# The last layer of a four-layer image network turned round: transposes behind the product, 8x8 patches as partitions, border columns moved by DMA and added by VectorE

## What is computed

```python
# layer 3, x: B x 48 x 256 x 256, _gn: group norm (scale and shift folded into w_in here)
y = einsum('oc,bchw->bohw', w_in, _gn(x))                 # 48 -> 288 channels
yp = y cut into 8 x 8 patches                             # 32 x 32 patches an image
yp = irfft2(rfft2(yp) * fft_mask)                         # per channel, within a patch
y  = depthwise 3 x 3 convolution of the image put together again, zero border
x1, x2 = split(y, 2, axis=1)                              # 144 + 144 channels
out = x + einsum('oc,bchw->bohw', w_out, gelu(x1) * x2)   # 144 -> 48 channels
```

## Time and profile before

| | us |
|---|---|
| median of 3 runs | 12443.44 |
| lowest, highest | 12438.75, 12449.53 |
| span of the profiled execution (no other time is given of it) | 12461.3 |
| of it TensorE busy | 12084.7 (97%) |
| of it VectorE, ScalarE, GpSimd busy | 7757.3, 5633.1, 4999.7 |

### The profile page before, as it was taken

One profiled execution on the slowest core, in us unless ns is written; L12 is line 12 of the kernel. 1 busy time (PEld: TensorE's weight loads), 2 busy tenths in 40 slices (PEclk: granted clock), 3 DMA queues, 4 the chain that ended last, 5 costly groups with the idle time before them and its releaser, 6 DMA issues. The chain is left out here.

```text
span 12461.3 us, 389987 instructions
## 1 busy us (share of the span) xinstructions
PE 12084.7 (97%) x160850; PEld 8648.5 (69%) x160850; DVE 7757.3 (62%) x17493; ACT 5633.1 (45%) x11858; POOL 4999.7 (40%) x4364
## 2 busy tenths in 40 slices
PE   8999999899989999899999999999998999999999
PEld 7877444499977777555555555555557888888887
DVE  0000455444435545788888888888887777777777
ACT  0000111243433333455555555555556777777776
POOL 0000222212420055566666666666663444444444
PEclk9999999999999999999999999999999999999999
DMA  4333465695984587766666666666662222222222
GB/s 142 132 132 132 127 159 154 147 179 89 166 164 146 147 230 199 93 88 87 88 89 88 88 88 88 88 88 87 89 87 67 57 57 57 57 54 56 55 55 52
DMA packets 2289545, 1323.30 MB, mean 106 GB/s; under 512 B 1876085, under 2 KB 2199164, under 8 KB 2202256
## 3 DMA queue, kind: packets, MB, share of 16 engines
q1 hardware_dynamic: 2013196, 1200.80, 49.5%
q10 hardware_dynamic: 275072, 105.14, 3.7%
HBM read 648.82 MB, written 450.45 MB: 88 GB/s over the span
## 5 line engine op out<-in xcount | busy, mean ns | idle before, releaser
L1803 PE MATMUL l_m<-l_wa,l_pix 128*128 128x288 f32 x8192 | 2211.4, 413 | 2.7 <-DVE l_wb L1985 2.7
L1803 PEld LDWEIGHTS l_m<-l_wa,l_pix 128*128 128x128 f32 x8192 | 1475.5, 190 | 688.8 <-issue 361.9
L1659 POOL TENSOR_TENSOR l_qkv<-l_qkv,l_copies 128x576 f32<-128x576 f32 x1024 | 1437.1, 1403 | 631.3 <-DVE l_qkv L1996 621.5
L1649 POOL TENSOR_TENSOR l_pix<-l_raw 128x516 f32<-128x516 f32 x1024 | 1217.1, 1189 | 1042.6 <-DVE l_t L2033 1017.1
L1484 PE MATMUL l1h_ps<-l1h_ring,l1h_w 96*96 96x256 f32 x6120 | 1328.8, 379 | 62.7 <-ACT l1h_ring L1426 60.2
L1484 PEld LDWEIGHTS l1h_ps<-l1h_ring,l1h_w 96*96 96x96 f32 x6120 | 999.8, 163 | 391.5 <-issue 60.4
L2318 PEld LDWEIGHTS l_e<-k_ident,l_turn 128*112 128x112 f32 x9900 | 1069.1, 133 | 173.0 <-issue 110.6
L2318 PE MATMUL l_e<-k_ident,l_turn 128*112 128x128 f32 x9900 | 1158.2, 275 | 11.4 <-ACT l_turn L2403 3.0
L2403 ACT ACTIVATE l_spread<-l_e 112x512 f32<-112x512 f32 (+1 forms) x1584 | 871.7, 569 | 521.4 <-PE l_e L2318 509.5
L1517 DVE SCALAR_TENSOR_TENSOR l1h_ring<-l1h_ps,l1h_bias,l1h_columns 96x256 f32<-96x256 f32 x1020 | 670.4, 657 | 678.4 <-PE l1h_ps L1484 672.7
L517 PE MATMUL l0a_rows<-l0a_x 128*49 128x245 f32 x8144 | 1043.0, 371 | 0.0
(11 more groups left out here) (269 smaller groups left out, 22947.3 us busy)
## 6 DMA issues: line engine op xcount, KB each, us to landing
l0a_x<-x_px_dram SPq DMA_DIRECT2D x128, 1176.0 KB, 5.1
l0b_x<-x_in_dram SPq DMA_DIRECT2D x128, 493.8 KB
l_raw<-l_raw SPq DMA_DIRECT2D x128, 483.6 KB, 7.3
l_raw<-x_dram SPq DMA_DIRECT2D x1270, 48.0 KB, 3.7
l_x<-x3p_dram SPq DMA_DIRECT2D x132, 384.0 KB
l_out<-x_dram SPq DMA_DIRECT2D x528, 96.0 KB, 2.4
out_dram<-l_out SPq DMA_DIRECT2D x132, 384.0 KB, 4.5
x_dram<-l0b_out ACTq DMA_DIRECT2D x256, 193.5 KB, 3.1
```

Source lines behind the costliest of these rows:

```text
L1649: nc.gpsimd.tensor_tensor(pix[:, n % 2, i, half * HALF:(half + 1) * HALF].rearrange("p (r w) -> p r w", w=PW), in0, in1, op).then_inc(pix_ ...
L1659: nc.gpsimd.tensor_tensor(q, q, copies[:, g % 2, 1:2, :].broadcast_to([128, 2, OUTC]), ALU.add)\
L1803: last = nc.tensor.matmul(bank[i][:, 0:OUTC], pix[:, k, i, first:first + 128], wa[:, b, i, :], start=True, stop=(i in (1, 2)))
```

## The change

The product is left as it is, but what follows it is turned round: patches stay partitions through the rim sums, gelu and the product of the halves, and the transposes come last.

- `turn` is now two buffers of 128 partitions (two parts of the channels x 64 patches) by 10 x 10 positions by 2 halves by 24 channels, and positions run along the free axis.
- The border columns lie in neighbouring partitions now. `move_edges` has SP copy them by DMA: for each of the four groups of 32 partitions and each of two sides one transfer from `turn` to `edge`, shifted by one partition, so 31 partitions of 480 values (1920 bytes) each; 8 transfers a third, 24 a band. `add_edges`, on DVE, adds both sides in one instruction.
- GpSimd only adds and saves the border rows, 128 x 768 each; the four short adds a third are gone.
- gelu and the product are two pieces a third (128 x 768) instead of four of 112 x 512. The product goes to `gate`, from which 16 transposes a third (not 50) are made, behind it; ACT alone copies them (`read_rows`, 4 of 128 x 512 a third, in place of the 13).
- `project` is one step a band, of 6 x 4 x 2 = 48 products of 24 rows by 512 columns, not two steps of 12 with 48 rows.
- The constants come without the old permutation of channels.

Cut to its core:

```diff
+            def move_edges(n, j):
+                u = n * 3 + j
+                sp.wait_ge(a_out, conv_at(n, j, COMP))
+                sp.wait_ge(b_out, conv_at(n, j, COMP))
+                if u >= 2:
+                    sp.wait_ge(edged, u - 1)
+                for first in range(0, 128, TX):
+                    here, there = slice(first, first + TX - 1), slice(first + 1, first + TX)
+                    for side, column, dst, src in ((0, 9, there, here), (1, 0, here, there)):
+                        sp.dma_start(edge[dst, u % 2, side, :],
+                                     turn[src, u % 2, column].rearrange("p y g i -> p (y g i)")).then_inc(edge_in[u % 2], 16)
...
             def slab(q, ty, n, first, last):       # SP
                 if not last:
                     load_x(...)
+                move_edges(n, 0)
+                move_edges(n, 1)
                 if not first:
-                    store(n)
+                    store(n - 1)
+                move_edges(n, 2)
                 load_residual(q, ty, n, first)
...
             def slab(q, ty, n, first, last):       # TensorE
                     convolve(n, j)
-                    if j < 2 and not first:
-                        project(n, j)
-                    if j == 2 and not last:
-                        channels(nq, n + 1, False)
-                    transpose(n, j, first)
+                    if j == 0 and not first:
+                        transpose(n - 1, 2, False)
+                    if j == 1:
+                        if not first:
+                            project(n - 1, False)
+                        transpose(n, 0, False)
+                if not last:
+                    channels(..., n + 1, False)
+                transpose(n, 1, last)
...
+            def add_edges(n, j):                    # VectorE
+                u = n * 3 + j
+                tile = turn[:, u % 2].rearrange("p x y g i -> p x (y g i)")
+                dve.wait_ge(a_out, conv_at(n, j, COMP))
+                dve.wait_ge(b_out, conv_at(n, j, COMP))
+                dve.wait_ge(edge_in[u % 2], 128 * (u // 2) + 128)
+                nc.vector.tensor_tensor(tile[:, 1:9:7], tile[:, 1:9:7], edge[:, u % 2], ALU.add).then_inc(edged, 1)
...
             def slab(q, ty, n, first, last):        # VectorE
+                for g in range(COMP):
+                    read_turn(dve, nc.vector.tensor_copy, 1, n, 0, g, b_done, b_out)
+                    if g in (1, 3) and not first:
+                        gated(u - 1, g // 2)
+                for g in range(COMP):
+                    read_turn(dve, nc.vector.tensor_copy, 1, n, 1, g, b_done, b_out)
+                    if g == 1:
+                        add_edges(n, 0)
+                for h in range(2):
+                    gated(u, h)
+                add_edges(n, 1)
+                if not first:
+                    for m in range(4):
+                        residual(n - 1, m)
+                for g in range(COMP):
+                    read_turn(dve, nc.vector.tensor_copy, 1, n, 2, g, b_done, b_out)
+                ...
+                    for g in range(YR):
+                        read_y(dve, nc.vector.tensor_copy, 1, n + 1, g, False, b_done, a_done, b_out)
+                        if g == 5:
+                            add_edges(n, 2)
+                        if g in (4, 7):
+                            gated(u + 1, g // 7)
...
         def _(pool):
-            def join(pairs):
-                s = spread[:, pairs]
-                nc.gpsimd.tensor_tensor(s[:, :, 8, :, 0:TX - 1], s[:, :, 8, :, 0:TX - 1], s[:, :, 0, :, 1:TX], ALU.add)
-                nc.gpsimd.tensor_tensor(s[:, :, 1, :, 1:TX], s[:, :, 1, :, 1:TX], s[:, :, 9, :, 0:TX - 1], ALU.add)
+                    pool.wait_ge(edged, u + 1)
```

More of the change, by code:

```diff
@@ L2116, in stage_l3 @@
     AB = YR + 3 * COMP
[L2117 to L2125, removed]
+    EDGE = 10 * C
+    LANE = 32
+    GROUPS = PX // 4
     with nc.cleanup_on_exit(), ExitStack() as ctx:
@@ new lines, in project @@
+            def project(n, ended):
+                pe.wait_ge(t_out, n * 12 + 12)
+                bank_pair_read(conv_at(n, 2, 5) if ended else conv_at(n + 1, 1, 2))
+                for k in range(6):
+                    j, r = k // 2, k % 2
+                    for m in range(4):
+                        lanes = slice(m * LANE, m * LANE + CH)
+                        for side in range(2):
+                            last = nc.tensor.matmul(e[m][side * HI:side * HI + C, :], wout[lanes, j, r, :],
+                                                    rows[lanes, j, side * 8:(side + 1) * 8, r, :], start=(k == 0), stop=(k == 5),
@@ L2394, in turned_before @@
-        def turned_before(eng, n, j, first):
-            if not (first and j == 0):
-                for k in range(2):
-                    eng.wait_ge(e_done[k], (n * 3 + j) * E[k])
+                    if j == 0 and not first:
[5 more added lines that the diff above has]
+                if not last:
+                    channels(1 if q == 0 and ty == BANDS - 1 else q, n + 1, False)
@@ new lines, in slab, with read_y @@
+                transpose(n, 1, last)
+            slabs(slab)
+            transpose(N - 1, 2, True)
+            project(N - 1, True)
+        def read_y(eng, copy, s, n, g, first, done, other, ready):
+            if g == 0 and not first:
+                eng.wait_ge(other, n * AB)
+            eng.wait_ge(done, n * AB + (g + 1))
+            bank = slots[MIX_SLOTS[g % 4]][s]
+            m0 = s * TX + STARTS[g]
+            copy(y[:, :, m0:m0 + SIZES[g]], bank[:, 0:SIZES[g] * C3].rearrange("p (t c) -> p c t", c=C3)).then_inc(ready, 1)
@@ L2439, in _ @@
+                if last:
+                    for h in range(2):
+                        gelu(u + 1, h)
+                else:
+                    for g in range(YR):
+                        read_y(act, copy, 0, n + 1, g, False, a_done, b_done, a_out)
+                        if g in (3, 6):
+                            gelu(u + 1, g // 6)
+                read_rows(n, 1)
             slabs(slab)
-            for piece in range(4):
-                gelu(2 * BANDS - 1, 2, piece)
+            for h in range(2):
+                gelu(N * 3 - 1, h)
@@ L2476, in residual @@
[L2476 to L2482 removed]
+            dve.wait_ge(blank, 1)
+            dve.sem_inc(blank, 1)
+            for g in range(YR):
+                read_y(dve, nc.vector.tensor_copy, 1, 0, g, True, b_done, a_done, b_out)
```

407 lines of the change are left out of this document (171 added, 236 removed).

## The result

The changed kernel takes 15,973.0 us (median of 4 runs, 15,959.1 to 15,978.0), the kernel before, run beside it, 12,446.5 (12,438.8 to 12,452.1): a ratio of 1.283, 95% interval 1.281 to 1.285. The forecast was 15,930. The profiled execution spans 15,976.0 us.

A forecast was written before the change was run, and what follows sets the result against it. Three serial waits for single-engine edge transfers bound a band: 3 x 23.2 + 23.6 + 5 (clock) = 98.2 us against 45.3; +52.9 over 66 bands adds 3490, giving 15,930 us, range 14,800 to 17,600.

The forecast's parts named there:

- One engine for 31 partitions: Edge transfers: equal shares of partitions put all eight of a set through one DMA engine, 21.1 us a set.
- L: Time from a third's last copy to its landed edges, three times a band: 23.2 us each (20.0 to 33.6).
- Rival 1: Edge pieces spread over all DMA engines, issues bound a set: L 4.6 to 6.7 us, 12,130 us, faster; chance 0.09.
- Rival 2: Each edge transfer has one engine, but a set's eight have different ones: 49.8 us a band, 12,740 us; chance 0.06.
- The piece's time: Edge transfers: one engine takes 85 ns for each 1920-byte piece, with 72 and 127 as ends.
- rival 3: The single engine copies edge pieces at 127 ns: some 17,600 to 18,200 us; chance 0.08.
- Three waits, none beside another: DVE's in-order queue keeps a band's three edge waits from overlapping, so a band lasts at least three times L plus the rest.
- Between the waits: Band work outside the three edge waits: 23.6 us at full clock plus 5 for the clock, 28.6 in all.
- The clock behind the second wait: TensorE's products after edges 1 start at half speed following the pause, adding 2.5 us a band.
- The last part: Edges 2 landed to third 0's last copy in the next band: 5.7 + 6.4 us, plus 1.7 for the clock.
- What the engines alone would allow: Last layer, if only busy times counted: a band falls from 45.3 to about 32 to 37 us.
- The sign for the DMA engines: Last layer's profile: mean share of the DMA engines stays low, near 7% for the edges plus 11 for the rest.

The follow-up runs named there:

- e1: Changed kernel with 30 partitions per edge transfer instead of 31, the last pair of patches of each group left out: 13,245.6 us, ratio 1.064 to the kernel before.
- e2: Changed kernel with each 31-partition edge transfer split into two, of 16 and 15, so sixteen a set: 14,291.4 us, ratio 1.147 to the kernel before.
- e3: Changed kernel with edge transfers of 112 and 15 partitions per side, a mask in VectorE's sums removing cross-strip pairs: 12,612.2 us, ratio 1.013 to the kernel before.
- e5: Changed kernel, same 31-partition transfers, but the wait and the edge sum moved from VectorE's queue to GpSimd's: 14,432.1 us, ratio 1.160 to the kernel before.
- e9: Changed kernel plus 165 and 130 unused identity transposes on TensorE in the waits for edges 0 and 1: 15,945.7 us, ratio 1.280 to the kernel before.
- e4: Changed kernel without the edge transfers and VectorE's wait for them, the sum adding zeros: 12,254.6 us, ratio 0.984 to the kernel before.
- e10: e4 also without the loads of x behind the first band, all bands reading the first band's x: 12,088.3 us, ratio 0.970 to the kernel before.
- e7: e3 with the edge sums placed later in VectorE's queue, behind other copies and the residual: 12,289.1 us, ratio 0.987 to the kernel before.
- e6: Changed kernel with GpSimd adding the edges and ten transfers a set, of 64 and 15 partitions: 12,599.5 us, ratio 1.012 to the kernel before.

## Why the prediction was right

**One engine for 31 partitions: right.** It was read off a share of 45.0% for loads of 49 partitions. After the change the share is 6.6% and the pieces go one at a time. e1 (30 partitions), e2 (16 and 15) and e3 (112 and 15) each cut L, from 22.5 us to 8.7, 13.9 and 5.7 on the mean, with the same or nearly the same bytes. The rule quoted from the Trainium skill ("DMA: Bandwidth & Descriptors", section "Why a DMA increments its semaphore by 16 and not by 1") agrees with all four in how many engines share a transfer; which engines they are, no run shows. Rival 1 (spread, 12,130) and rival 2 (different engines for the eight, 12,740) are refuted by the 1.04 above.

**The piece's time: 79 ns, taken as 85.** It lies near the row of one engine's share that I chose; rival 3's 127 ns, from rows of 16 engines at once, did not come. The first two waits are 1.4 us shorter for it, and the third is 24.0, since the loads of the residual (L2216) are issued while its set is under way: in the set above the step from one piece of the edges to the next is 99 ns from the first of the residual's pieces on, where it was 83 until then. I had said that none of SP's other transfers was in front of a set, which holds; that one could lie beside it I had not counted. The three waits are 2.2 us a band shorter than forecast.

**Three waits, none beside another: right, for the reason given.** TensorE has 64 long waits of each of the three kinds in 64 bands. e5 shows that the order on VectorE makes them add up: off its queue, the same transfers cost 23 us a band less.

**Between the waits: 2.7 us a band too low.** 31.3 us on the mean (4.2 + 10.7 + 16.3) against 28.6, and 32.6 in the band above. That the sum, 98.2, came within 0.5 us of the mean band is luck in part: this error and that of the three waits are of one size and cancel.
- The residual was mis-sized: 4.04 us for four sums, taken as 4 x 0.69 = 2.8 from a line of before. It did not lengthen its part, because TensorE starts after two of the four: the chain has two sums, 2.07 us from 12069.26, and then TensorE at 12071.37. The two that were left out of the path take off more (1.4 us at the forecast's price) than the longer ones put on (0.7 for two).
- The clock behind the second wait was sized right: from 12071.37 to the last copy it is 6.8 us, less 0.7 for that copy 6.1, for which 3.55 + 2.5 were taken. That this adds up is luck in part, since the low clock and the residual's last two sums lie beside each other: the sums end at 12073.30 and TensorE's second group starts at 12073.35, so at full clock the first group would have gained nothing, as e9 shows. Three windows of the changed kernel show 15 us without a product, then the two levels, 0.50 (1.2 GHz) and 1.00:

```profile
12056.00:12071.00 15.00, 0.00 (x0) 0.00 (x0) 2.82 (x3) 0.24 (x1) 1.58 (x1) 0.55 0.05 19
12071.00:12073.00 2.00, 1.63 (x40) 1.63 (x40) 2.00 (x3) 0.00 (x0) 1.07 (x2) 0.50 0.03 8
12075.00:12078.00 3.00, 3.00 (x141) 3.00 (x136) 2.53 (x4) 2.51 (x4) 0.00 (x0) 1.00 0.69 180
```

- The last part was mis-sized most, 16.3 on the mean against 13.8. In the band above it is 18.4, and a stop of TensorE of 3.6 us stands in it, 4.6 us after the loads of x are issued at 12106.23, of the kind that e4 has and that shrinks in e10. Over all bands the stops in this part that follow a fetch come to 2.2 us on the mean, and the part is long where they are long (correlation 0.85 over 62 bands). So the stops are in it; that the loads of x cause them here too is a likeness, not a test, since the changed kernel was not run without them.

```profile
12106.43 1.94 PE l_e L2318 x8
12110.82 3.62 issue
12114.45 2.11 PE l_e L2296 x65
```

**`project`: eight side by side, right.** The profile has two matrix instructions for each product, and at full clock 94 of the 96 for the 48 products take 5.31 us (e4's chain); four at a time was to be 10.6. In the changed kernel it lasts 7 us, partly at the half clock, beside a wait.

**What the engines alone would allow: wrong, and without effect here.** I gave 32 to 37 us a band "if only busy times counted", and e4, which comes nearest to it, has 42.2. TensorE is busy for 35.4 of them and not 32, and it stops for some 7, of which the stops that follow an instruction fetch take some 4 us a band and the waits for the residual 1.2. Had rival 1 been the case, its 12,130 would have been missed by far more than its range of L: e3 is that case with an L of 5.7 us, and it takes 12,612. The point from which the change is a gain is not L = 7.2 us, as I wrote, but (45.3 - 31.4) / 3 = 4.6 with what lies between the waits in e1, and 5.0 with the 30.2 of e3, which stands on the far side of it.

**The sign for the DMA engines: wrong in its sum.** I wrote a mean share near 7% for the edges plus 11 for the rest. One engine of 16 is near 7% only while a set is under way, 60 of 98.7 us, so it should have said 4 plus 11; the windows have 0.15.

Why the kernel before, with the same loads of x, has so few of these stops (23 us of stops that follow a fetch between 9600 and 12000, against 226 in e4) stays open.

## What to carry to other kernels

Before a transfer is put on the path, factor its partition count: a shift by one within 32 partitions moves 31, and 31 went through one DMA engine at 79 ns for each 1920 bytes, 20 us where a masked shift of 112 and 15 partitions took 3.8. Then look at what stands behind the waiting instruction on its engine: the same transfers cost 23 us a band less on an idle engine's queue (e5), and the short ones of e3 cost 5 us a band less where the wait was placed behind the work that did not need it (e7), next to nothing over a run without transfers. And sum the bound from a run without the suspected cost, not from busy times: here that sum was 5 to 10 us a band too low.

## What the runs showed that I had not expected

- In the changed kernel, where all transfers of a set go to one engine, the later issues of a set take longer: 0.60 us the first, 1.64, 2.07 and 2.42 the last three on the chain. There the one engine's work hides that. Where the work is spread, the count of partitions shows in the issue too: transfers of 16, 64 and 112 partitions take 0.53 to 0.60 us (medians, e2, e6, e3), as the 0.57 of the earlier trace rows, but those of 15 and 30 take 0.78 to 0.84 (e1, e2, e3, e6). In e1 and e2 the issues are most of the wait.
- The residual's sum of 512 values takes 1.08 us where it took 0.69 before. What changed is how it steps through its tiles: it now reads and writes `out` with a step of four values (L2485, `[..., m]`), where it went through `out` value by value and through `l_e` with a step. No run here separates the cause.
- TensorE stops for 1 to 5 us at a time for nothing that the profile names, and nearly all the long stops end just after 16,384 bytes have landed on the instruction queue, 4.0 us a band in e4 by those that follow a fetch; most of the stops of over 2 us went when the loads of x were left out.
